# A search of the 31 largest: three of eight units, in place of two, end with a masked copy made on GpSimd

## The reference

```
x = x + 0.5 * ffn(layernorm(x))     # block "b" in the kernel
x = x + attn(layernorm(x))
x = x + 0.5 * ffn(layernorm(x))     # block "a" in the kernel

attn: 16 heads of 16 channels; U = int(5 * log(512)) = 31
  scores = Q K^T / 4                               # 512 x 512 for each head
  thresh = the 31st largest score of each row
  scores = where(scores < thresh, -inf, scores); softmax; times V; times Wo

ffn: a gate gives each token weights over 16 experts (those with a positive
  logit, or the best two if none has one); q, k, v = weighted sums over experts;
  causal attention over 512 tokens, width 64; weighted sum of expert outputs
```

## Time and profile before

| | us |
|---|---|
| median of 3 runs | 4824.97 |
| lowest and highest | 4823.51 and 4827.64 |
| the profiled execution, its own time | 4825.1 |
| its span, first to last instruction | 4823.0 |
| busy: DVE, PE, ACT, POOL | 4405.2, 4138.3, 3608.2, 3374.2 |

### The profile page before, as it was taken

The page is one execution under the profiler, slowest core; times in us unless marked ns, Lnnn a source line. Parts: engine busy times, 40 slices in busy tenths (PEclk is TensorE's granted clock), DMA queues, the critical chain, the costliest instruction groups (busy, mean ns, idle before and its releaser), DMA issues.

```text
span 4823.0 us, 121133 instructions
## 1 busy us (share of the span) xinstructions
PE 4138.3 (86%) x33100; PEld 3408.1 (71%) x33100; DVE 4405.2 (91%) x10326; ACT 3608.2 (75%) x9285; POOL 3374.2 (70%) x4822
## 2 busy tenths in 40 slices
PE   5767889998998989889898989989898889977776
PEld 4555777777777777777777777777777777766555
DVE  0199999999999999999999999999999999999980
ACT  2367778877887887878777887878787787877662
POOL 5555777777777777777777777777777777754544
PEclk8888999999999999999999999999999999999888
DMA  3201111111212121111112111211111121111011
GB/s 85 52 21 32 47 53 50 52 52 48 53 49 54 49 52 49 53 51 50 53 47 54 49 52 49 54 49 49 54 47 54 49 53 49 52 38 26 21 30 49
DMA packets 244186, 232.98 MB, mean 48 GB/s; under 512 B 27123, under 2 KB 176628, under 8 KB 243316
## 3 DMA queue, kind: packets, MB, share of 16 engines
q1 hardware_dynamic: 243444, 224.49, 17.4%
HBM read 214.98 MB, written 9.44 MB: 47 GB/s over the span
## 4 chain that ended last, share of the span: by engine, by line
issue 54%; DVE 28%; PE 7%; DVEq 4%; POOL 3%; ACT 2%; SPq 0%; POOLq 0%; DMA 0%; ACTq 0%
DVE M L866 14%; DVE W L868 10%; PE pQ L531 4%; DVEq L275 4%; DVE M L873 3%; POOL HS L970 2%; DVEq L279 1%; PE pST L516 1%; ACT S L743 0%; DVE mxr_a L846 0%; ACT S L773 0%; DVE mxr_b L846 0%; POOL mixT L988 0%; ACT OUT L769 0%; PE pFa L418 0%
## 5 line engine op out<-in xcount | busy, mean ns | idle before, releaser
L531 PE MATMUL pQ<-wf_sb,HS 128*128 128x192 f32 x8192 | 1587.7, 352 | 455.1 <-POOL HS L970 454.0
L866 DVE MAX8 M<-W 128x8 f32<-128x512 f32 x2816 | 1810.9, 680 | 41.6 <-DVE W L868 6.0
L531 PEld LDWEIGHTS pQ<-wf_sb,HS 128*128 128x128 f32 x8192 | 1459.1, 206 | 537.5 <-POOL HS L970 414.2
L868 DVE MATCH_REPLACE8 W<-M,W 128x512 f32<-128x512 f32 x1792 | 1197.8, 674 | 0.0
L1007 POOL TENSOR_SCALAR LM<-S,M 128x512 bf16<-128x512 f32 x256 | 517.7, 2022 | 503.7 <-DVE M L866 324.7
L550 PE MATMUL pST<-ident,S 128*128 128x128 f32 x4096 | 747.2, 283 | 12.6 <-ACT S L743 12.6
L769 ACT ACTIVATE OUT<-S,M 128x512 bf16<-128x512 f32 x1024 | 750.1, 733 | 6.2 <-DVE W L868 4.9
L773 ACT ACTIVATE S<-S,M 128x512 f32<-128x512 f32 x1024 | 743.8, 726 | 0.0
L552 PE MATMUL pST<-steep,OUT 128*128 128x128 bf16 x4096 | 731.3, 222 | 0.0
L868 DVE MATCH_REPLACE8 W<-M,S 128x512 f32<-128x512 f32 x1024 | 683.7, 675 | 0.0
L866 DVE MAX8 M<-S 128x8 f32<-128x512 f32 x1024 | 650.9, 677 | 23.4 <-issue 22.6
(11 more groups left out here) (230 smaller groups left out, 6343.1 us busy)
## 6 DMA issues: line engine op xcount, KB each, us to landing
RB<-rows_b SPq DMA_DIRECT2D x384, 256.0 KB, 3.3
RB<-rows_a SPq DMA_DIRECT2D x384, 256.0 KB, 3.3
x_b<-in_x SPq DMA_DIRECT2D x64, 128.0 KB, 2.9
out_y<-y SPq DMA_DIRECT2D x64, 128.0 KB, 2.7
wf_sb<-in_wf SPq DMA_DIRECT2D x4, 768.0 KB, 7.2
rows_b<-rwT_b SPq DMA_DIRECT2D x64, 8.0 KB, 1.3
wof_sb<-in_wof SPq DMA_DIRECT2D x1, 1024.0 KB, 7.2
rows_a<-rwT_a SPq DMA_DIRECT2D x64, 8.0 KB, 1.4
```

Of the source, the lines that this page charges most:

```text
L531: mm = nc.tensor.matmul(pQ[:, 0:QKV], HS[:, k % 2, e, i, :], wf_sb[:, i, at:at + QKV], start=k + e + i == 0, stop=(k, e, i) == (3, 3, 1))
L866: nc.vector.max(m, src[i]).then_inc(s_tk, 1)
L868: nc.vector.match_replace(W[:, i, :], m, src[i], -BIG).then_inc(s_tk, 1)
```

## The change

`LIGHT` becomes three units of a gang of eight, (1, 3, 5), in place of one unit of four, which is two of eight. `GANG` takes the place of the number 4 in the places that count them. Everything else follows from these numbers: unit 3 of each eight loses its sixth and seventh pass and gets `LM`, `XL`, a count, a MAX8 over `XL` and the picking. The slots of each step are as they were relative to the pair of the unit. ACT's count gets a further wait, for the previous count, since the counts all write the same `spare`.

```diff
-LIGHT = (1,)
+GANG = 8
+LIGHT = (1, 3, 5,)
 FOUND = 8 * (ROUNDS - 1)
-ORDER = [(p, i, k) for p in range(2) for k in range(PASSES) for i in range(2) if k < PASSES - 2 or 2 * p + i not in LIGHT]
+ORDER = [(p, i, k) for p in range(GANG // 2) for k in range(PASSES) for i in range(2) if k < PASSES - 2 or 2 * p + i not in LIGHT]
...
 def passed(w, c, k):
-    p, i = c % 4 // 2, c % 2
-    return w.count(QUADS * len(ORDER), c // 4 * len(ORDER) + ORDER.index((p, i, k)) + 1)
+    p, i = c % GANG // 2, c % 2
+    return w.count(SPAN // GANG * len(ORDER), c // GANG * len(ORDER) + ORDER.index((p, i, k)) + 1)

 def light(w, j, slot):
     for k, u in enumerate(LIGHT):
-        if at := due(w, j, slot + u // 2 * 2, 4, QUADS * NB):
+        if at := due(w, j, slot + u // 2 * 2, GANG, SPAN // GANG * NB):
             n, c = at
-            return n * len(LIGHT) + k, c * len(LIGHT) + k, 4 * c + u
+            return n * len(LIGHT) + k, c * len(LIGHT) + k, GANG * c + u
...
                 if at := light(w, j, LCNT):
                     n, c, u = at
+                    wait(act, s_lcnt, n)
                     wait(act, s_lpos, n - 1)
                     held(act, s_low, n + 1)
...
-                    if c % 4 in LIGHT:
-                        held(act, s_lth, w.count(QUADS * len(LIGHT), c // 4 * len(LIGHT) + LIGHT.index(c % 4) + 1))
+                    if c % GANG in LIGHT:
+                        held(act, s_lth, w.count(SPAN // GANG * len(LIGHT), c // GANG * len(LIGHT) + LIGHT.index(c % GANG) + 1))
...
-                        if p != c % 2:
+                        if p != c % (GANG // 2):
```

## The result

| | median us | runs | ratio to before, 95% interval |
|---|---|---|---|
| before | 4826.31 | 4 | |
| changed | 4883.0 (4867.56 to 4891.16) | 4 | 1.0117 (1.0101 to 1.0132) |

A forecast was written before the change was run, and what follows sets the result against it. DVE was taken to bound the kernel, with POOL, PE and ACT adding no cost. From 4825.1 us, 128 light units at 0.42 us took 54, giving 4771 us; own range 4764 to 4782, whole range 4760 to 4810.

The forecast's parts named there:

- DVE sets the pace, a third light unit saves 54 us: DVE's list: 128 more light units each drop one MATCH_REPLACE8, net 0.42 us each, 54 us in all.
- The price of the lone MAX8: DVE, light pair: the partner's MAX8 waits for its own MATCH_REPLACE8, costing 0.23 us more than an interleaved one.
- POOL at 87%, in step again within the gang: POOL: 4.3 us more per gang raises it from 75% to about 87%; its idle time absorbs the delay.
- the second place: Slot 16 (0): HS ends by 2518.0, PE comes only at 2519.82, so no cost; cover given as over 1.9 us.
- Cover left: 3.5 us, so the cost is nothing: Slot 8: HS 3.2 us later, score copies done at 2491.2, DVE wants them at 2494.7, so no cost.
- PE's 1.9 us of delay: Slot 8: HS ends at 2484.0 where PE began at 2482.10, so PE starts 1.9 us late.
- The signs of being wrong: DVE idle ahead of a pair's first MAX8 or the one over XL, or its durations growing, would refute the prediction.
- no new wait: ACT: unit 1's held threshold ran at 2482.46, picked would be done at about 2481.3, so nothing is added.
- DVE runs dry: Rival at the first pair of 16: late HS plus lower clock make DVE wait 2.8 us, 64 times; 4950 us, 9%.
- its decision point of 0.84 us in 16 units: DVE's wait at the first pair of 16 above which the kernel becomes slower.
- The port: Rival: POOL's 3.2 us of LM and XL hold up DVE, 410 us less 54; 5181 us, 1%.

The follow-up runs named there:

- e6: Changed kernel with LM and XL behind the ffn steps of their slot, and count, picking and threshold one slot later: 4777.26 us, ratio 0.9897.
- e2: Changed kernel with unit 3's LM and XL made for only 64 of 512 columns, part of the computation left out: 4785.57 us, ratio 0.9919.
- e9: Changed kernel with 15 constant multiplications ahead of PE's wait for the HS of slot 8, in two of four tiles: 4828.26 us, ratio 1.0010.
- e10: Changed kernel with count, picking and threshold one slot later, LM and XL still ahead of the ffn steps: 4805.69 us, ratio 0.9954.
- e11: The order of e6 with only units 1 and 5 of eight light: 4820.24 us, ratio 0.9993 to the kernel before.
- e7: Changed kernel with only units 1 and 5 of eight light, as before the change: 4821.27 us, ratio 0.9993.
- e3: Kernel before with four additional POOL operations of 128x256 in each slot 8 of 8: 4857.71 us, ratio 1.0073.
- e4: Changed kernel with ffn a's softmax statistics one slot later, the reduce behind the pair of slot 12: 4801.27 us, ratio 0.9945.
- e5: Changed kernel with 24 constant multiplications ahead of PE's wait for the HS of slot 8: 4967.77 us, ratio 1.0294.

## Why the prediction was wrong

- **DVE sets the pace, a third light unit saves 54 us: right.** e6 and e2, with the waits gone, are 49 and 40 us under before, and e6 lies 6 us over the 4771 forecast. The price of the lone MAX8 (0.23 us) held: the new pairs last 8.29 us, 7.69 and a MAX8.
- **POOL at 87%, in step again within the gang: right in size.** 1704 us of 2000, 85%; `HS` of slot 8 ended 14.1 us ahead of DVE's turn for the reduce before and 10.7 after (median), nearly as worked out (3.2 and DVE's 0.42); that of slot 10 came 1.2 us nearer and that of slot 12 0.8. Two readings were off without harm: the pair of slot 8 starts 1.0 us earlier, not 0.42, since the pair ahead of it is shorter by 1.0 and the MAX8 over `XL` comes behind it; and the cover at the second place is 1.8 us by the prediction's own times, not over 1.9.
- **"Cover left: 3.5 us, so the cost is nothing": the step that failed.** It followed one user of the late chain, the copies into `S`, to DVE's pair of slot 12. ACT's next copy in slot 11, `Sr_a`, is also wanted by DVE, and earlier, by the reduce between the two pairs. Its cover was 2.0 us before (done at 2492.80 for a reduce at 2494.82), 1.6 with DVE's gain. PE's 1.9 us of delay alone went past it, and the reduce waits 0.7 us on average in this kind of tile, with no lower clock in any. Besides, the tile that was read is one kind of four: there PE came to `HS` 1.4 us after it was ready; in two of the other kinds it came at once (3.0 us after the pair's start, as `HS` did), so all 3.2 us reached it, on a cover of 3.1 to 3.3; there the clock fell in all but one tile, and the reduce waits 2.4. The row had no idle time before the change, so no view of waits showed it; only a walk over all that DVE takes from others would have. The signs of being wrong did not name it either: they named a pair's first MAX8 and the one over `XL`, and DVE's idle time came ahead of the reduce.
- **The lower clock stood in the wrong place.** The text had the price, 2.4 us for a chunk at 1.2 GHz, but gave it to a rival at another pair, though its own numbers put 3.2 us of new idle time in front of PE in slot 8. e9 shows that this was over half of the loss.
- **ACT: "no new wait".** Nearly true of ACT (26.4 us ahead of the threshold, 22.9 before), but its further threshold in slot 11 delays the copy behind it; e10 shows that ACT's count and threshold ahead of that copy matter, 0.8 us in each tile.
- **The rival "DVE runs dry"** named the mechanism (late `HS`, lower clock, DVE waits) and its decision point of 0.84 us in 16 units; measured 1.4 (89.3 us over 64). Its place was wrong, a pair's first MAX8 in place of the reduce, and it got 9%.
- **The port: right.** MAX8 from `S` lasts 678 ns on average, 677 before, with POOL 15% busier. By the narrower rule of the Trainium skill ("SBUF — State Buffer", section "SBUF: two separate sides"), under which GpSimd holds up a DVE operation only if that has two SBUF inputs or uses both ports, nothing else was due.
- **Open:** the 12 us more at the turn of the loop. Kernels with a full pair at the end of the loop have 19.8 (e11), 20.0 (e7) and up to 26.9 us (e3) there; those with a light pair have 20.9 (e4) to 41.1 us (e10), so the light pair alone does not explain it. It was not taken further.

## What to carry to other kernels

Before work is put onto an engine with spare time, list everything that the bounding engine takes from others, small in-order steps too, and the time by which each is early; the smallest of these is the cover, not that of the main data. In an in-order queue the place decides: the changed kernel took 57 us more than before with the copy ahead of a product that others wait for, and 49 less (e6) with the copy behind it and the count and picking a slot later. And price new idle time of TensorE with the chunk behind it at the lower clock.

## What the runs showed of the hardware

- TensorE's clock turned a wait into a larger one: in the changed kernel PE idled 3.4 to 3.8 us ahead of the chunk of slot 8 in 28 tiles, the granted clock fell in 27 of them shortly before or after the chunk's start, and 2.77 us of work took 4.3 to 5.5. With 0 to 2.1 us of idle time there it fell in 2 of 26 tiles; in e3, behind 2.6 to 3.1 us, in 19 of 27. So the length of this idle time alone did not decide. Constant multiplications in the idle time kept the clock up in the tiles that had them and were worth 55 us net.
- A 128x128 f32 multiplication shows as two instructions and takes 0.23 us in a row (24 in 5.5 us), twice the 0.12 us that the expectation of e5 had.
